# Moving three blocks of record scatters behind the first expert gathers on GpSimd

## The reference, cut to what matters

```
x = x + relu(segment_sum(edge_weight * (layernorm(x) @ W)[dst], src) + bias)   # 16384 edges
xt = layernorm(x)
scores = sigmoid(xt @ Wg.T + bg);  w, idx = top_k(scores, 2);  w = w / w.sum(-1)
nx = (xt - mean) * rsqrt(var + eps)
for each expert e, for the tokens that chose it:
    h = silu((gamma*nx + beta) @ W1[e] + b1[e]) * ((gamma*nx + beta) @ W3[e] + b3[e])
    y += w * (h @ W2[e] + b2[e])
z = (silu(nxs @ Ws1 + bs1) * (nxs @ Ws3 + bs3)) @ Ws2 + bs2,  nxs = nx*gs + bs
x = x + y + z
```

## Time and profile before

| | |
|---|---|
| device time, median of 3 runs | 434.47 us |
| device time of the profiled execution | 434.47 us |
| its span | 432.7 us |
| TensorE busy | 396.9 us (92%) |
| VectorE busy | 212.7 us (49%) |
| ScalarE busy | 156.6 us (36%) |
| GpSimd busy | 174.4 us (40%) |
| DMA moved | 129.15 MB |

### The profile page before, as it was taken

One profiled execution on the slowest core, in us unless ns is written; L12 is line 12 of the kernel. 1 busy time (PEld: TensorE's weight loads), 2 busy tenths in 40 slices (PEclk: granted clock), 3 DMA queues, 4 the chain that ended last, 5 costly groups with the idle time before them and its releaser, 6 DMA issues.

```text
span 432.7 us, 6405 instructions
## 1 busy us (share of the span) xinstructions
PE 396.9 (92%) x1898; PEld 207.9 (48%) x1899; DVE 212.7 (49%) x696; ACT 156.6 (36%) x387; POOL 174.4 (40%) x275
## 2 busy tenths in 40 slices
PE   6799999999999998999999999997978867898985
PEld 5467768665655556444344344343433333343431
DVE  8999998136566676642332332331232223112447
ACT  8687786322233120323233233231321231132232
POOL 2779995315655676332332232231131122121100
PEclk9999999999999998999999999998999999898999
DMA  7999960400004572599999999999999999999378
GB/s 270 217 379 409 405 253 3 143 25 26 24 24 139 229 284 89 208 406 405 403 407 407 409 405 406 408 405 408 406 405 409 406 408 405 407 397 373 140 274 313
DMA packets 44022, 129.15 MB, mean 298 GB/s; under 512 B 8054, under 2 KB 9270, under 8 KB 43858
## 3 DMA queue, kind: packets, MB, share of 16 engines
q1 hardware_dynamic: 38242, 120.45, 72.8%
q0 software_dynamic: 5744, 8.28, 5.4%
HBM read 119.64 MB, written 17.85 MB: 318 GB/s over the span
## 4 chain that ended last, share of the span: by engine, by line
PE 78%; issue 7%; DVE 5%; POOL 4%; DMA 3%; SPq 1%; ACT 1%; DVEq 0%; ACTq 0%; POOLq 0%
PE bank L1476 27%; PE bank L1339 13%; PE bank L1506 12%; PE bank L1498 5%; PE bank L1288 4%; PE bank L1464 4%; PE bank L1261 3%; DMA w<-totals 2%; PE bank L1327 2%; PE bank L1360 2%; POOL M L500 1%; POOL AT L500 1%; PE bank L1233 1%; PE bank L1348 1%; DVE stats L812 1%
## 5 line engine op out<-in xcount | busy, mean ns | idle before, releaser
L1133 DVE SCALAR_TENSOR_TENSOR osl<-bank,b13T,osl 128x64 f32<-128x64 f32 x128 | 27.5, 277 | 158.5 <-ACT osl L734 158.5
L1476 PE MATMUL bank<-w,xhT 128*64 128x512 f32 x352 | 84.0, 619 | 13.9 <-issue 13.9
L727 ACT COPY xh<-bank 128x512 f32<-128x512 f32 x33 | 19.3, 585 | 142.0 <-PE bank L1476 135.9
L1339 PE MATMUL bank<-HW,AT 128*128 128x512 f32 x128 | 58.2, 593 | 0.0
L1476 PEld LDWEIGHTS bank<-w,xhT 128*64 128x64 f32 x352 | 25.9, 141 | 56.8 <-issue 55.3
L594 POOL DMA_INDIRECT totals<-GW,A x16 | 16.4, 1023 | 84.6 <-PE bank L1464 70.3
L594 POOL DMA_INDIRECT totals<-osl,A x16 | 16.4, 1026 | 77.4 <-PE bank L1464 69.6
L1506 PE MATMUL bank<-w,osl 128*64 128x512 f32 x176 | 41.8, 594 | 0.5 <-DVE osl L1133 0.5
L590 POOL DMA_INDIRECT A<-nx_rows,A x33 | 34.2, 1035 | 12.3 <-issue 9.7
L1339 PEld LDWEIGHTS bank<-HW,AT 128*128 128x128 f32 x128 | 22.9, 191 | 21.0 <-issue 21.0
L643 ACT ACTIVATE osl<-iota,eT 128x128 f32<-128x128 f32 x90 | 27.8, 387 | 10.1 <-PE bank L1288 10.1
(11 more groups left out here) (238 smaller groups left out, 595.0 us busy)
## 6 DMA issues: line engine op xcount, KB each, us to landing
w<-in_L_ffn_W_dram SPq DMA_DIRECT2D x66, 1024.0 KB
A<-in_L_ffn_W_dram SPq DMA_DIRECT2D x15, 1024.0 KB
HW<-in_L_ffn_W_dram SPq DMA_DIRECT2D x10, 1024.0 KB
AT<-in_L_ffn_W_dram SPq DMA_DIRECT2D x5, 1024.0 KB
totals<-w SPq DMA_DIRECT2D x1, 4096.0 KB, 25.8
w<-totals SPq DMA_DIRECT2D x8, 512.0 KB, 7.2
out_dram<-X SPq DMA_DIRECT2D x8, 256.0 KB, 2.3
X<-in_x_dram SPq DMA_DIRECT2D x3, 512.0 KB, 7.5
```

The lines of the kernel that those rows point to most:

```text
L1133: ins = v.scalar_tensor_tensor(hT[b][:, m, CAP * h:CAP * h + CAP], bank[4][:, (HC + m) * P + CAP * h:(HC + m) * P + CAP * h + CAP], b13T[: ...
L1339: ins = t.matmul(bank[4 + s % 2][:, :], AT[:, s % 2, k, :], HW[:, k, :], start=(k == 0), stop=(k == NB - 1))
L1476: ins = t.matmul(bank[2 + b][CAP * h:CAP * h + CAP, :], xe[b][:, c, CAP * h:CAP * h + CAP], up_w[v][:, h, :, c, :], start=(c == 0), stop=( ...
```

## The change

The loop over blocks scatters the records of blocks 0 to 4 alone. The wait for list_in and the scatters of blocks 5 and 6 leave it, and with those of block 7 they come behind the four gathers and behind stacked(7). The number of instructions is unchanged: six indirect DMAs and one wait stand elsewhere in GpSimd's order.

```
@@ in the loop over s (blocks)
                 if s >= 1:
                     stacked(s - 1)
-                if s >= 1:
-                    if s - 1 == DRAM_BLOCKS:
-                        pool.wait_ge(list_in, 16)
+                if 1 <= s <= DRAM_BLOCKS:
                     scatter_records(s - 1)
             values(NB - 1)
@@ after the loop
             pool.wait_ge(list_ready, 1)
             for j in range(AHEAD):
                 gather(TOK[:, j:j + 1], j)
-            scatter_records(NB - 1)
             stacked(NB - 1)
+            pool.wait_ge(list_in, 16)
+            for s in range(DRAM_BLOCKS, NB):
+                scatter_records(s)
             pool.wait_ge(zero_out, 16)
```

## The result

The changed kernel took 436.37 us (median of 10 runs, 435.52 to 436.77) against 433.52 us (431.42 to 435.37) for the kernel before on the same chip: ratio 1.0061, 95% interval 1.0041 to 1.0082. It is slower, by 2.6 us (1.8 to 3.6). The forecast was 434.6 us and no change, with 435.8 us as the most that the terms of the sum could add up to. The profiled execution took 438.14 us, above all of these ten runs; a second profile further down took 436.19 us and shows the same picture, so I rest the account on both.

A forecast was written before the change was run, and what follows sets the result against it. The prediction took the weight stream to bound the second half. Its terms, -0.05 + 0.07 + 0.11 = +0.13 us on 434.47, gave 434.6 us, with a range of 434.0 to 435.4.

The forecast's parts named there:

- What bounds the kernel: Second half: runs at the speed of the weight stream, so its end is its start (176.76 us) plus bytes over rate.
- What the change removes: GpSimd at 152 to 163 us: four scatters and a wait leave; path gain 0, less disturbance perhaps 0.05 us.
- Place 1: VectorE line 1155 beside stacked(7): slowed by GpSimd's instructions there, taken as 0.07 us, between 0 and 0.29.
- Rival A: At line 1155 the port blocks VectorE, costing 0.29 us: 434.8 us in all; chance 0.15.
- Place 2: Weight stream after 178.6 us: about four scatters take its DMA time, 0.11 us, at most 1.04.
- Place 3: Gather of pair 4, issued about 181.9 us: in at 188.5, wanted by TensorE at 190.87; cover 2.4 us, cost 0.
- Place 4: Scatter of pair 0 at 184.90 us: GpSimd is free at about 183.2, cover 1.7 us, cost 0.
- Rival B: GpSimd's queue slow beside the full stream, pair 4's gather late: 440.4 us, milder form 435.5 to 435.8; chance 0.09.
- Rival C: Transposes of line 1233 at 165.87 us: clock may stay high, stream starts up to 1 us earlier, 433.5 us; chance 0.07.

The follow-up runs named there:

- e2: The kernel before without its scatters of blocks 5, 6 and 7 and without the wait on list_in: 434.33 us, ratio 1.0015.
- e12: The changed kernel itself run once more, unaltered, for a second profile: 436.06 us, ratio 1.0046 to the kernel before.
- e4: The kernel before with only the two scatters of block 7 put behind stacked(7): 434.31 us, ratio 1.0006.
- e6: The changed kernel with its six late scatters turned into indirect reads of the same slots into an unused tile: 435.07 us, ratio 1.0037.
- e3: The changed kernel with the gather of pair 4 put ahead of the six scatters: 436.89 us, ratio 1.0080.
- e7: The changed kernel with its six scatters together in round 10 of GpSimd's loop, SyncE's further-chunk read moved to round 13: 434.55 us, ratio 1.0036.

## Why the prediction was wrong, point by point

**What bounds the kernel: right.** The reading that the weight stream sets the second half, so that DMA time lost after 178.6 us is lost for good, is what turned a stall of some 3 us into a slower kernel.

**What the change removes: right, gain 0.** Line 545 starts 0.28 us after line 988 began (156.56 against 156.28) as before, values(7) still follows VectorE's line 1014, and the gathers still wait for line 1042. e2 measured the same from the other side.

**Place 1, VectorE beside stacked(7): smaller than taken.** Line 1155 after:

```profile
172.47 0.42 DVE L1155 TENSOR_TENSOR xhT<-xhT,bT 128x256 f32<-128x256 f32 x1
```

0.42 us as in the earlier trace rows; in this profile the term of 0.07 us was 0. It was GpSimd that gave way: its line 568 took 0.35 instead of 0.29 us and line 570 took 0.57 instead of 0.43. That is in line with the rule of the Trainium skill, SBUF — State Buffer, "Who interferes with whom", that the later of the two waits, though by 0.06 to 0.14 us and not for a whole instruction: VectorE had started first both times. Where VectorE came second it gave way. In e12, the same kernel, the second line 1155 started 0.05 us behind GpSimd's line 569 and took 0.56 us; in e4, while GpSimd issued a gather, the first took 0.61. So the size of the term was sound, and the 0 is in part luck. Rival A is out: at 434.8 us it could not have made the 436.4, and e12's first line 1155, the one on the path, took 0.43.

**Place 2, the DMA time of the scatters: the step that failed.** I priced four scatters at 0.11 us and at most 1.04. The changed kernel lost 1.30 MB, 3.2 us by its profile and 2.6 us by its times. The term priced each scatter by the share its own packets hold, from a row where the engines were idle; the upper bound came from a gather's share, the same kind of number. That kind measures what the small DMAs occupy, and it came out right (0.10 us). It cannot hold what they do to the packets of another queue, whose mean time rose from 0.16 to 1.2 us. The one thing that changed the nature of the load, six issues in a row beside a full stream, occurs nowhere in the kernel before: its scatters go in pairs, and its longest row of indirect DMAs, at 166 to 174 us, runs while the stream is still. There was no row to price it by, and I should have said so and left more chance to it.

The rule in the Trainium skill, DMA: Bandwidth & Descriptors, "Specifications", that transfers under 512 bytes are read-modify-writes, pointed to the slower side, and I set it aside. No run here shows that it is the mechanism: e6 writes nothing to DRAM and still loses 1.6 us, but its reads are of 8 bytes too.

**Place 3, the gather of pair 4: wrong in time, right in cost.** Its lag was 10.2 us (issued 182.53, TensorE released at 192.76), not 6.6, and the cover of 2.4 us was overrun by 1.02 us. As worked out there, a delay under 1.6 us starves nothing; e3 confirmed it.

**Place 4: right.** The scatter of pair 0 started at 185.59, still waiting for its result.

**Rival B** named the slower side and GpSimd's queue behind the filled stream, at 0.09. Its mechanism, TensorE waiting for the gather, is refuted by e3. Its milder form was the upper bound of place 2, 1.04 us and 435.8 us; the side was right and the size was not, since that bound was a share as well.

**Rival C** happened, in part, and was outweighed. It holds that the clock may be high ahead of the transposes, so that the first gather ends the wait instead. The granted clock in 166 to 167 us was 0.50 in the kernel before, 0.55 in the first profile after and 1.00, the upper level, in the second (e12), where TensorE then waited 0.77 us for the first gather. It moved the first load by 0.36 us between two executions of one kernel, so it is not an effect of the change.

## What to carry to other kernels

Before moving small DMAs "off the path", look at what the DMA engines do at the place they go to: with a stream that bounds the kernel, six of them in a row cost 2.6 us, and the same six in pairs 5 us apart, or ahead of the stream, cost nothing that can be measured. Judge a DMA beside a stream by the GB/s of the stream, not by the share of its own packets or by the engines' busy share, which stayed at 0.98 over 7 us while the rate fell to 249 GB/s. And where the trace before has no stretch in which the new load exists, an upper bound taken from shares is no bound.

## What the runs showed of the hardware

- Six indirect DMAs of 128 records of 8 bytes, issued 1.3 us apart beside a stream of 406 GB/s, take it down to 60 and 108 GB/s over 3 us (two profiles of the same kernel); the mean time of a packet of the stream rises from 0.16 us to 1.2 us in one of them (packets of 185 to 186 us) and to 0.6 us in the other (184.5 to 185 us). Four give 306 GB/s over the same 3 us. Reads in place of writes cost 1.6 us, but in their profile the stream ran empty.
- Beside the stream, the packets of the third scatter came some 4.5 us after its issue (177.48, then 182 to 183 us); before it, those of the first two were done within 2 us. A gather behind the six landed 10.2 us after its issue.
- The breakdown comes late: in e7 the six were issued from 246.3 to 253.7 us and the rate fell in 255.6 to 258 us.
- In e7 TensorE stood still through 256 to 258 us, and the granted clock was 0.52 of 2.4 GHz, close to its lower level of 1.2 GHz, in the next 2 us and 0.50 until 264 us. What it waited for was ScalarE's copy, which started at 258.06, 4.6 us later behind the matmuls than the round before it:

```profile
246.97 0.58 ACT L728 COPY xh<-bank 128x512 f32<-128x512 f32 x1 [3.15 <-PE bank L1477]
258.06 0.58 ACT L728 COPY xh<-bank 128x512 f32<-128x512 f32 x1 [7.78 <-remote]
```

  The timed loss of 1.6 us is no more than the 1.9 us that the bytes say, so nothing shows that this stop added to it.
